# Expert inner rows in chunks of 128, 128, 128 and 64 instead of four chunks of 112

## The reference, cut to what matters

```python
scores = softmax(xf @ gate_w);  _, sel = top_k(scores + expert_bias, 2)      # 8 experts
routed_in = xf[token_idx] * top_scores_sorted[:, None]
h = silu(ragged_dot(routed_in, w1, counts)) * ragged_dot(routed_in, w3, counts)
routed_out = ragged_dot(h, w2, counts)        # w1, w3: 8 x 512 x 448   w2: 8 x 448 x 512
out = silu(xf @ sw1) * (xf @ sw3) @ sw2       # the shared expert, same widths
out = out.at[token_idx].add(routed_out)
```

## Time and profile before

| | us |
|---|---|
| median of three runs | 1342.69 |
| the profiled execution's own time | 1343.7 |
| its span, first to last instruction | 1342.0 |
| TensorE busy in the span | 1256.9 |
| VectorE busy | 656.1 |
| ScalarE busy | 446.4 |
| GpSimd busy | 407.3 |

### The profile page before, as it was taken

The page is one execution under the profiler, slowest core; times in us unless marked ns, Lnnn a source line. Parts: engine busy times, 40 slices in busy tenths (PEclk is TensorE's granted clock), DMA queues, the critical chain, the costliest instruction groups (busy, mean ns, idle before and its releaser), DMA issues.

```text
span 1342.0 us, 18348 instructions
## 1 busy us (share of the span) xinstructions
PE 1256.9 (94%) x6226; PEld 1062.6 (79%) x6227; DVE 656.1 (49%) x1104; ACT 446.4 (33%) x755; POOL 407.3 (30%) x333
## 2 busy tenths in 40 slices
PE   4999989999999999999999998999999999999960
PEld 3788878878888888888888877888788888888850
DVE  6555257544365655755456457766232232223216
ACT  3333342233234433343244346552222222222210
POOL 2221112000013211221234224247866240017854
PEclk9899999999999999999999999988999999999995
DMA  6822267553658875784866421045636242224457
GB/s 204 274 79 64 83 232 266 185 222 135 251 196 310 291 287 185 282 323 170 267 254 219 159 73 54 28 159 213 213 121 188 78 161 78 74 73 156 142 161 254
DMA packets 88395, 240.42 MB, mean 179 GB/s; under 512 B 8300, under 2 KB 35144, under 8 KB 76040
## 3 DMA queue, kind: packets, MB, share of 16 engines
q1 hardware_dynamic: 64824, 160.19, 33.1%
q0 software_dynamic: 23040, 79.08, 18.3%
q10 hardware_dynamic: 464, 0.27, 0.1%
HBM read 163.75 MB, written 75.76 MB: 178 GB/s over the span
## 4 chain that ended last, share of the span: by engine, by line
PE 87%; DVE 5%; DMA 2%; POOL 2%; issue 2%; ACT 1%; POOLq 0%; ACTq 0%; DVEq 0%
PE bank L1176 26%; PE bank L1346 19%; PE bank L1204 13%; PE bank L1384 10%; PE bank L1101 4%; PE bank L1121 4%; PE bank L1313 2%; PE bank L1131 2%; PE bank L1364 1%; POOL fin_low L784 1%; PE bank L1148 1%; DVE xres L1937 1%; DVE wl L1523 1%; PE bank L1087 1%; DMA yg<-y_sorted,slot 1%
## 5 line engine op out<-in xcount | busy, mean ns | idle before, releaser
L1176 PE MATMUL bank<-xTh,G 128*128 128x512 f32 x1024 | 278.6, 397 | 1.8 <-DVE xTl L1629 1.8
L1176 PEld LDWEIGHTS bank<-xTh,G 128*128 128x128 f32 x1024 | 188.8, 188 | 42.5 <-issue 3.4
L1346 PE MATMUL bank<-W,dxh 128*128 (+2 forms) x880 | 205.8, 376 | 8.4 <-DVE dmid L1783 5.1
L1346 PEld LDWEIGHTS bank<-W,dxh 128*128 128x128 f32 x880 | 164.2, 191 | 23.8 <-issue 8.5
L1204 PE MATMUL bank<-DN,bhh 128*128 128x512 f32 x512 | 158.0, 390 | 0.0
L1176 PE MATMUL bank<-xTl,G 128*128 128x512 f32 x512 | 137.4, 390 | 0.0
L1384 PE MATMUL bank<-W,dhh 112*128 (+1 forms) x440 | 126.1, 408 | 1.8 <-ACT dys L994 1.8
L1651 DVE SCALAR_TENSOR_TENSOR bs<-bank,tab,bs 128x512 f32<-128x512 f32 x64 | 47.5, 742 | 161.1 <-PE bank L1176 161.1
L1783 DVE TENSOR_TENSOR dmid<-bank,dsg 128x448 f32<-128x448 f32 x55 | 34.2, 622 | 173.9 <-ACT dsg L984 173.9
L1204 PEld LDWEIGHTS bank<-DN,bhh 128*128 128x128 f32 x512 | 96.2, 188 | 21.3 <-issue 1.7
L1176 PEld LDWEIGHTS bank<-xTl,G 128*128 128x128 f32 x512 | 96.1, 188 | 20.7
(11 more groups left out here) (250 smaller groups left out, 1989.6 us busy)
## 6 DMA issues: line engine op xcount, KB each, us to landing
G<-gate_up_split SPq DMA_DIRECT2D x48, 1024.0 KB, 7.0
DN<-down_split SPq DMA_DIRECT2D x24, 1024.0 KB, 4.9
wst<-in_L_ffn_w POOLq DMA_DIRECT2D x24, 896.0 KB, 5.9
gate_up_split<-G SPq DMA_DIRECT2D x16, 1024.0 KB, 7.3
y_all<-dys SPq DMA_DIRECT2D x55, 256.0 KB, 2.0
xs_sorted<-zero POOLq DMA_DIRECT2D x3, 3328.0 KB, 20.7
xsd<-xs_sorted SPq DMA_DIRECT2D x39, 256.0 KB, 3.0
down_split<-DN SPq DMA_DIRECT2D x8, 1024.0 KB, 3.9
```

The costliest lines, as they stand in the source:

```text
L1176: mm = pe.matmul(bank[m][:, :], G[:, c % 2, f, h, m, i, :], a[b % 2][:, i, :], start=(n == 0), stop=(n == 3 * DC - 1))
L1346: mm = pe.matmul(bank[o][:, 0:width], a[par][:, k, :], w[:, bass.ds(slot, 1), at + k * step:at + k * step + width].rearrange("p a n -> p ( ...
```

## The change

The 448 inner rows stand as three full chunks of 128 (`HF` = 3) and a rest of 64 (`HR`). The fourth chunk holds the 64 rows twice: in partitions 0 to 63 the high half, in 64 to 127 the low half. Its weights are laid out twice too, so that one product of 128 rows gives high by high and low by high for the rest.

- `w2` and `sw2` are handed in as 128 partitions of four rows (`packed_down`), the last 64 rows twice. Loads, casts and subtractions of `w2` cover 128 partitions instead of 112.
- `d_mul` becomes two instructions: 384 columns, and the last 64 columns written twice (128).
- `d_mid` transposes four pieces of 128 columns.
- ScalarE's `d_hid` copies 128 partitions instead of 112.
- VectorE's `d_hid` becomes two: 128 partitions by 384 columns into `dhl`, and partitions 64 to 127 of the fourth chunk, 64 by 128, in place into `dhh`.
- `d_down` has 11 products: three `dhh` by `Wh`, three `dhl` by `Wh`, the mixed fourth, three `dhh` by `Wl`, and last one of 64 rows (`dhh` by `Wl`, the rest).

```diff
-            ("dhh0", [HP, HC, P], F32R), ... ("dhl0", [HP, HC, P], F32R), ...
+            ("dhh0", [P, HC, P], F32R), ... ("dhl0", [P, HF, P], F32R), ...
@@ ScalarE d_hid
-                act.activation(dhh[t % 2]..., bank[1][0:HP, :], ACT.Copy).then_inc(s_dhh, 1)
+                act.activation(dhh[t % 2]..., bank[1][:, :], ACT.Copy).then_inc(s_dhh, 1)
@@ TensorE d_mid
-                    mm = pe.transpose(bank[1][0:HP, k * P:(k + 1) * P], dmid[par][:, k * HP:(k + 1) * HP], ident)
+                    mm = pe.transpose(bank[1][:, k * P:(k + 1) * P], dmid[par][:, k * P:(k + 1) * P], ident)
@@ TensorE d_down
-                n = 0
-                for a, w in ((dhh, Wh), (dhl, Wh), (dhh, Wl)):
-                    if n == HC:
-                        pe.wait_ge(s_dhl, t + 1)
-                    if n == 2 * HC and not shared:
-                        pe.wait_ge(s_w2, e + 2)
-                    for k in range(HC):
-                        mm = pe.matmul(bank[4][:, :], a[par][:, k, :], w[0:HP, ...], start=(n == 0), stop=(n == 3 * HC - 1))
-                        n += 1
-                mm.then_inc(s_dd, 1)
+                def part(a, w, k, q, start=False, stop=False):
+                    return pe.matmul(bank[4][:, :], a[par][0:q, k, :], w[0:q, ...], start=start, stop=stop)
+                for k in range(HF):
+                    part(dhh, Wh, k, P, start=(k == 0))
+                pe.wait_ge(s_dhl, t + 1)
+                for k in range(HF):
+                    part(dhl, Wh, k, P)
+                part(dhh, Wh, HF, P)
+                if not shared:
+                    pe.wait_ge(s_w2, e + 2)
+                for k in range(HF):
+                    part(dhh, Wl, k, P)
+                part(dhh, Wl, HF, HR, stop=True).then_inc(s_dd, 1)
@@ VectorE d_mul
-                dve.tensor_tensor(dmid[t % 2][:, :], bank[3][:, 0:HID], dsg[:, :], ALU.mult).then_inc(s_dmid, 1)
+                full = HF * P
+                dve.tensor_tensor(dmid[t % 2][:, 0:full], bank[3][:, 0:full], dsg[:, 0:full], ALU.mult)
+                dve.tensor_tensor(dmid[t % 2][:, full:].rearrange("p (a n) -> p a n", n=HR),
+                                  bank[3][:, full:HID].unsqueeze(1).broadcast_to([P, 2, HR]),
+                                  dsg[:, full:].unsqueeze(1).broadcast_to([P, 2, HR]), ALU.mult).then_inc(s_dmid, 1)
@@ VectorE d_hid
-                dve.tensor_tensor(dhl[t % 2]..., bank[1][0:HP, :], f32(dhh[t % 2]...), ALU.subtract).then_inc(s_dhl, 1)
+                dve.tensor_tensor(dhl[t % 2]..., bank[1][:, 0:HF * P], f32(dhh[t % 2][:, 0:HF, :])..., ALU.subtract)
+                dve.tensor_tensor(dhh[t % 2][HR:P, HF, :], bank[1][HR:P, HF * P:HC * P],
+                                  f32(dhh[t % 2][HR:P, HF, :]), ALU.subtract).then_inc(s_dhl, 1)
@@ layout of w2 and sw2
+def packed_down(a):
+    k, p = np.arange(HC)[None, :], np.arange(P)[:, None]
+    return a[..., np.where(k < HF, k * P + p, HF * P + p % HR), :]
```

More of the change, by code:

```diff
@@ L44 @@
 HC = 4
-HP = HID // HC
+HF = HID // P
+HR = HID - HF * P
 HELD = 8
@@ L374, in program @@
         shared_part = (sw1.rearrange("(k p) n -> p k n", p=P), sw3.rearrange("(k p) n -> p k n", p=P),
-                       sw2.rearrange("(k p) n -> p k n", p=HP))
+                       sw2)
         router = gate_w.rearrange("(k p) n -> p k n", p=P)
         def w_rows(p, width, at=None):
-            q, step = ((P, G_W), (P, HID), (HP, D))[p]
-            return wst[p if at is None else at][0:q, 0:HC * step].rearrange("p (k n) -> p k n", k=HC)[:, :, 0:width]
+            step = (G_W, HID, D)[p]
+            return wst[p if at is None else at][:, 0:HC * step].rearrange("p (k n) -> p k n", k=HC)[:, :, 0:width]
         def turn_of(kind, t):
@@ L562, in w_part @@
                     return shared_part[p]
-                w, q = ((w1, P), (w3, P), (w2, HP))[p]
-                return w[bass.ds(idx - 1, 1), :, :].rearrange("e (k p) n -> p (e k) n", p=q)
+                if p == 2:
+                    return w2[bass.ds(idx - 1, 1), :, :, :].rearrange("e p k n -> p (e k) n")
+                return (w1, w3)[p][bass.ds(idx - 1, 1), :, :].rearrange("e (k p) n -> p (e k) n", p=P)
             places = [0]
@@ L579, in w_place @@
             def w_place(whole, slot, p, width):
-                q, at, step = ((P, W_1, G_W), (P, W_3, HID), (HP, W_2, D))[p]
-                return whole[0:q, slot, at:at + HC * step].rearrange("p (k n) -> p k n", k=HC)[:, :, 0:width]
+                at, step = ((W_1, G_W), (W_3, HID), (W_2, D))[p]
+                return whole[:, slot, at:at + HC * step].rearrange("p (k n) -> p k n", k=HC)[:, :, 0:width]
             def w_high(idx, p, slot):
@@ L988, in d_hid @@
                 wait(act, s_dd, t - 1)
-                act.activation(dhh[t % 2][:, :, :].rearrange("p k n -> p (k n)"), bank[1][0:HP, :], ACT.Copy).then_inc(s_dhh, 1)
+                act.activation(dhh[t % 2][:, :, :].rearrange("p k n -> p (k n)"), bank[1][:, :], ACT.Copy).then_inc(s_dhh, 1)
             def d_y(t):
@@ L1376, in d_down @@
                 wait(pe, s_dy, t)
[L1377 to L1388 removed]
+                def part(a, w, k, q, start=False, stop=False):
+                    return pe.matmul(bank[4][:, :], a[par][0:q, k, :],
+                                     w[0:q, bass.ds(slot, 1), W_2 + k * D:W_2 + (k + 1) * D].rearrange("p a n -> p (a n)"),
+                                     start=start, stop=stop)
+                for k in range(HF):
[9 more added lines that the diff above has]
+                part(dhh, Wl, HF, HR, stop=True).then_inc(s_dd, 1)
             for t in range(TT):
@@ L1982 @@
     for name in _INS:
-        a = _np.ascontiguousarray(inputs[name])
+        a = _np.asarray(inputs[name])
+        if name in LAYOUTS:
+            a = LAYOUTS[name](a)
+        a = _np.ascontiguousarray(a)
         arrays[f"in_{name}"] = a
```

10 lines of the change are left out of this document (6 added, 4 removed).

## The result

| | before | after |
|---|---|---|
| median, us | 1342.69 | 1350.46 |
| lowest and highest of 7 runs each | 1341.38, 1344.99 | 1345.85, 1351.37 |
| the profiled execution | 1343.7 | 1348.94 |
| its span | 1342.0 | 1346.9 |
| TensorE busy | 1256.9 | 1260.9 |

The ratio is 1.0047, 95% interval 1.0035 to 1.0059, which is 6.3 us (4.7 to 7.9): the kernel became 0.5% slower. The forecast was 1348.5 us, range 1333.5 to 1351.5, "slower" with 0.66. In the profile after, `d_down` is L1382, `d_mid` L1367, `d_up` L1349, `d_turn` L1316, `d_mul` L1793 and L1795, `d_hid` on VectorE L1801 and L1804.

What follows compares the result with a forecast made beforehand. TensorE was taken to bound the routed tiles, VectorE's chain and GpSimd's scatters parts of the shared one. Shifts of +1.86 us to 973 and +3.96 for tiles 16 to 51 gave +5.8 on 1342.69: 1348.5 us, range 1333.5 to 1351.5.

Steps and rivals of the forecast that it cites:

- One product less: TensorE, down products of each tile: twelve become eleven, -0.23 us a tile.
- The switch: TensorE, around the 64-row product: going to a 64-row array and back costs 0.19 + 0.15 = 0.34 us a tile.
- the sign to look for: Routed tile in the profile after: `dmid` to `xsd` transposes 3.34 us instead of 3.23, or 3.00 if the switch is free.
- Wider transposes and more rows: TensorE: `d_mid` at 128 columns and products of 128 rows for 112 cost 0, with 0.03 a tile kept either way.
- VectorE: Per tile `d_mul` +0.14 and `d_hid` +0.07 us, felt in the shared part and 0 in a routed tile.
- The shared part to 973: TensorE's shift, summed place by place from +0.28 us at 817 to +1.86 after the waits at 966 and 973.
- tile 16 waits for the scatters: TensorE at 956.13: a wait with 0.50 us to spare cuts the shift from +1.95 to +1.45.
- The routed part: Tiles 16 to 51: TensorE never kept waiting by what changes, 36 times 0.11 = +3.96 us.
- The end: GpSimd's wait for tile 51's store, at 1286.20 before, ends 5.8 us later.
- The switch costs nothing: Rival, TensorE: the 64-row array is free, -0.23 a tile, -8.6 us in all, 1334.1 us; chance 0.18.
- only the way in costs: Rival, TensorE: the way out is hidden, -0.04 a tile, -0.7 us in all, 1342.0 us; chance 0.12.
- VectorE makes the shared part slower still: Rival: `d_hid`'s second half and neighbours don't overlap, some six places at 0.15, +0.9 us, to 1349.4; no chance given.

Runs made afterwards that it cites:

- e1: Changed kernel with its last down product over 128 rows instead of 64: 8.31 us a routed tile; 1348.9 us against 1354.8 of the kernel before, ratio 0.9967.
- e3: Changed kernel with its last two down products at 64 rows: 8.68 us a routed tile, 1361.4 us against 1354.8 of the kernel before.
- e4: Kernel before with only its last down product cut from 112 to 64 rows: 8.91 us a routed tile, 1366.4 us against 1354.8, ratio 1.0090.
- e11: Changed kernel with its 64-row product moved to the middle of the down products: 8.69 us a routed tile.
- e5: Kernel before with VectorE's split instructions alone, all from partition 0: 8.56 us a routed tile, 1341.6 us.
- e8: Changed kernel with last product at 128 rows, SyncE's tile load ahead, low half's second instruction over all 128 partitions: 1329.9 us against 1342.7, ratio 0.9912.
- e6: Changed kernel with SyncE's tile load put ahead of its load of rows: 1345.5 us against 1342.6 of the kernel before, ratio 1.0021.
- e10: Kernel before with only SyncE's tile load put ahead of its load of rows: 1338.5 us against 1342.7, ratio 0.9974.

## Why the prediction was right, and where it was not

*One product less.* -0.23 a tile: from e1, 8.31 against 8.56 before, -0.25. Right to 0.02. That 64 rows are no cheaper than 128 by themselves: right, as one and two of them take the same (e3).

*The switch.* 0.34 was worked out from one product of 60 rows, two loads and a start. e4 has 0.35, e1 0.36, e11 0.38 (8.69 against 8.31). Per tile it gave +0.11, and 8.67 - 8.56 is that; the two terms are each 0.02 larger than I had them (-0.25 and +0.36), and that cancels. The distance `dmid` to `xsd` reads 3.28, not the 3.34 that I gave as the sign to look for: the other half shows behind the transposes' start, from where the next group follows after 0.41 (1158.26 to 1158.67) instead of 0.36. The tile was right, the place of the second half wrong.

*Wider transposes and more rows.* 0, and they are: with both, e1 is one product below the kernel before, to 0.02 us.

*VectorE.* `d_mul` +0.14, measured +0.13. `d_hid` +0.07 was **the term that was mis-sized**: +0.30. The note that the start at partition 64 may hold it was there, at 0.08 to 0.16, and left out of the sum. It shows in the shared part: from tile 0 to tile 2 the shift is +0.73 for the +0.28 foreseen, and to tile 8 +1.98 for some +1.1.

*The shared part to 973.* +1.86 foreseen from its start. Measured from tile 0 to tile 16 it is -1.36, and some +1.3 without the 2.7 us of the clock. That this is near is luck: by tile 8 the shift is already +1.98, since VectorE's share was too small, and the shorter second scatter, which I had not foreseen, takes 1.2 back. I also had a path wrong. The forecast let TensorE's shift be swallowed where "tile 16 waits for the scatters". In SyncE's queue the load of tile 16 also stands behind the store of tile 13, and in all 13 traces it is issued 0.63 to 0.64 us behind that store, while 3.9 to 12.6 us have passed since the last scatter. The store waits for ScalarE's copy of that tile's down bank, so it is TensorE's own chain that releases tile 16. In the traces before and after, the scatters hold TensorE only through the rows ahead of `dmid` of tile 11.

*The routed part.* 36 times 0.11 = +3.96; measured +3.9, as 35 distances at 0.11 and the first at 0.15, which has no `d_down` (e5 has 0.12 there from VectorE alone). **The step that failed** is the sentence that TensorE is never kept waiting there by what changes. It was read from TensorE's rows alone. Its three long tiles before (20, 30, 46) would have shown that the loads of `xsd` have no slack against VectorE's sum and SyncE's order, and VectorE's 0.43 us made a new one of 2.5 us: +1.5 in all.

*The end.* GpSimd's release 5.8 later was foreseen; +4.85 measured in the pair of traces. The forecast of +5.8 us stands against 6.7 by the traces at equal clock and 6.3 by the ratio. It is that near because the misses oppose each other: +0.9 too little for VectorE up to tile 8 and +1.5 too little for the long tiles, against tiles 8 to 11, where +0.3 was foreseen (+1.11 to +1.40) and -1.2 came with the shorter second scatter.

*The rivals.* "The switch costs nothing" falls with e4, "only the way in costs" with the second idle load of every tile. "VectorE makes the shared part slower still" was true up to tile 8 (+0.9, as it had it), and was named an addition rather than put in the sum, though the trace could not say which.

## What to carry to other kernels

Don't put a matrix product of 64 rows among products of 128: it costs 0.35 us in two crossings, more than the product itself (0.23), and padded to 96 or 128 rows it costs only its own time. What lies between 64 and 96 rows is not measured here. A load that feeds the bounding engine must not stand in its queue behind a wait for something that is not needed yet; the stalls that this makes come and go with shifts of 0.4 us elsewhere. An engine with idle time can still cost: compare not its busy share but what it releases. And a faster clock or a saved product ahead of a wait on another engine is given back there: compare two traces stretch by stretch, with the granted clock of each, before a row is put down to the change.

## What the runs showed of the hardware

- A load of weights that crosses between an array of 128 rows and one of 64 starts 0.07 us before the end of the product ahead, in both directions (e1 without it has 0.39), and a pair of crossings costs 0.35 to 0.38 us a tile (e4, e1, e11), for one product of 64 rows as for two (e3). 96 and 112 rows don't cross.
- A VectorE instruction of 128 columns on partitions 64 to 127 between two that start at partition 0 overlaps with neither: 0.90 us for the pair against 0.67 (e5) and 0.73 (e8).
- VectorE's three-operand sum in SBUF and GpSimd's subtraction in SBUF exclude each other: 0.74 us became 2.2 to 5.1 in the traces before, after and e6 when GpSimd was at work on the weights, and GpSimd's 4.60 became 5.09 when that started second.
- A 256 KB load issued 0.26 us behind a load of 1024 KB landed after 5.8 us, as did others issued 0.34 to 0.36 behind a load of weights; the median of such loads is 3.0.
- What TensorE gained by a higher clock was given back at its next wait on VectorE: with the granted clock from 885 to 900 us at 1.00 (e10) instead of 0.77 (before), the wait for `dmid` of tile 11 was 4.60 us instead of 2.78.
